# A gated Mamba block with a ternary feed-forward layer: the mean and variance of nine row tiles computed by ScalarE's accumulator in place of VectorE's batch-norm instructions

## What is computed

```python
def _layernorm(x, eps=1e-05):
    m = jnp.mean(x, axis=-1, keepdims=True); v = jnp.var(x, axis=-1, keepdims=True)
    return (x - m) / jnp.sqrt(v + eps)
# selective scan on ctx (4 x 512 x 256), gated by z = layernorm(x):
#   u = silu(causal_conv(ctx @ in_proj)), dt = softplus(...), B, C = rows of x_proj(u)
#   state = state * exp(dt * A) + (dt * u) * B ;  y = sum_n state_n * C_n  (16 states n, 512 channels)
x = x + tanh(g_xattn) * (y + D * u) * silu(z)
# ternary feed-forward layer, F = 2048: bitlinear(v, w) = quant8(rmsnorm(v)) @ ternary(w).T
h = silu(bitlinear(layernorm(x), w_gate)) * bitlinear(layernorm(x), w_up)
x = x + tanh(g_ffn) * bitlinear(h, w_down)
```

## Time and profile before

| what | us |
|---|---|
| three executions | 660.37, 652.05, 660.92 (median 660.37) |
| the profiled execution, whole time | 652.9 |
| its span, first to last instruction | 651.0 |
| what lies around the span | 1.9 |
| mean granted TensorE clock in it | 0.942 of full speed |

### The profile page before, as it was taken

How to read it: one execution, slowest core, us unless ns; L and a number is a source line. 1 busy time by engine, 2 the same in 40 slices (tenths; PEclk the granted TensorE clock), 3 DMA queues, 4 the chain that set the end, 5 groups by cost and what they waited for, 6 DMA issues and landing times. The chain is left out here.

```text
span 651.0 us, 9055 instructions
## 1 busy us (share of the span) xinstructions
PE 508.2 (78%) x2966; PEld 344.2 (53%) x2966; DVE 573.6 (88%) x796; ACT 501.3 (77%) x711; POOL 511.1 (79%) x281
## 2 busy tenths in 40 slices
PE   6998576876757577878778778787678777889996
PEld 2443264765645455656556556565456555654552
DVE  1879999999989999998989999999999999985642
ACT  3989699796977696969586868696878787766874
POOL 1534999999989999999999899999899989821000
PEclk9999777869788999899978998999998999999999
DMA  9993910711830101027301010183010010000000
GB/s 300 397 411 83 384 34 32 259 49 55 327 104 1 48 2 34 32 80 310 97 12 55 12 35 21 53 332 128 5 39 27 33 33 18 2 33 1 16 34 33
DMA packets 29985, 64.47 MB, mean 99 GB/s; under 512 B 3681, under 2 KB 11873, under 8 KB 26866
## 3 DMA queue, kind: packets, MB, share of 16 engines
q1 hardware_dynamic: 29938, 63.89, 27.4%
HBM read 55.75 MB, written 8.13 MB: 98 GB/s over the span
## 5 line engine op out<-in xcount | busy, mean ns | idle before, releaser
L669 POOL TENSOR_TENSOR area_s<-area_s,b_bc 128x1024 f32<-128x1024 f32 x128 | 300.7, 2363 | 21.6 <-DVE u_all L1159 16.9
L423 PE MATMUL pY<-ident,area_s 128*128 128x128 f32 x640 | 107.5, 296 | 81.2 <-DVE area_s L1167 79.9
L423 PEld LDWEIGHTS pY<-ident,area_s 128*128 128x128 f32 x640 | 76.5, 149 | 110.9 <-DVE area_s L1167 76.3
L878 ACT ACTIVATE pA<-dt_all,a_neg 128x512 f32<-128x512 f32 x160 | 107.8, 682 | 23.4 <-DVE area_s L1159 14.5
L463 PE MATMUL pG<-wq_gu,area_f 128*128 128x512 fp8e4 x448 | 112.6, 392 | 7.7 <-ACT area_f L844 5.6
L1159 DVE TENSOR_TENSOR_SCAN area_s<-pA,area_s 128x512 f32<-128x512 f32 x96 | 114.3, 1204 | 3.8 <-ACT pA L878 3.7
L1167 DVE TENSOR_TENSOR area_s<-area_s,pC 128x512 f32<-128x512 f32 x144 | 95.3, 664 | 9.8 <-issue 6.4
L661 POOL TENSOR_TENSOR u_all<-u_all 128x1024 f32<-128x1024 f32 x44 | 103.9, 2361 | 0.0
L417 PE MATMUL pC<-ident,xdT 128*128 128x128 f32 x576 | 94.5, 293 | 1.4 <-DVE xdT L1035 1.3
L417 PEld LDWEIGHTS pC<-ident,xdT 128*128 128x128 f32 x576 | 74.7, 150 | 6.1 <-DVE area_s L1167 3.4
L463 PEld LDWEIGHTS pG<-wq_gu,area_f 128*128 128x128 bf16 x448 | 43.5, 101 | 54.4 <-ACT area_f L844 7.6
(11 more groups left out here) (156 smaller groups left out, 960.0 us busy)
## 6 DMA issues: line engine op xcount, KB each, us to landing
b_bc<-bc_rows SPq DMA_DIRECT2D x16, 1024.0 KB, 7.5
area_s<-x SPq DMA_DIRECT2D x32, 256.0 KB, 3.0
u_all<-bc_rows SPq DMA_DIRECT2D x14, 512.0 KB, 5.9
b_bc<-w_gate SPq DMA_DIRECT2D x1, 4096.0 KB, 14.5
dt_all<-x SPq DMA_DIRECT2D x1, 4096.0 KB, 24.8
area_f<-w_up SPq DMA_DIRECT2D x1, 4096.0 KB, 34.2
area_f<-w_down SPq DMA_DIRECT2D x1, 4096.0 KB, 15.1
out<-area_f SPq DMA_DIRECT2D x16, 256.0 KB, 2.1
```

The lines of the kernel that those rows point to most:

```text
L423: mm = pe.matmul(pY[:, k * P:(k + 1) * P], src[:, k * P:(k + 1) * P], ident[:, :], is_transpose=True, start=(first and k == 0), stop=(last ...
L669: gp.tensor_tensor(db[c % NDB], du[s % 2].rearrange("p (a l) -> p a l", a=1).to_broadcast([P, CH, L]), b_bc[:, CH * c:CH * c + CH, :], ALU ...
L878: act.activation(exp_bank(s, n), dt_all[:, s, :], ACT.Exp, scale=a_neg[:, s % NT, n:n + 1]).then_inc(S["s_exp"], 1)
```

## The change

For nine tiles (t = 1, 2, 3, 5, 6, 7, 9, 10, 11) the statistics move from DVE to ACT. Tiles 0, 4, 8 and 12 to 15 keep `stats` on DVE (`own_stats`). For the nine:

- `x_sum(t)`, new: an ACT Copy over the 128 x 512 tile whose accumulator gives the sum. It stands at n = 3 of the step before the tile's own, and at n = 6 where t1 is a multiple of 4.
- `centre(t)` takes the sum as its bias and writes 512 times (mean - x). It moves from n = 10 to n = 8 (behind the two copies of hqT there), and stays at n = 10 where t1 is a multiple of 4.
- `x_deviation(t)`, new: an ACT Square over xn with accumulator, and a Copy of the 128 x 1 result with scale and offset into VE. It stands at n = 9, or at n = 10 right behind `centre`. The factor 512 cancels, since the root is of the scaled variance.
- `x_rstd(t)` on POOL moves behind `dt_u(s + 1)`, or behind `times_b(s + 1, 0)` where t1 is a multiple of 4, and waits for the new semaphore f_ve.
- The elementwise outputs of `x_sum` and `x_deviation` go to `nobody`, which is the space of w_xp_sb, used last in the first part of the kernel.

```diff
+def own_stats(t):
+    return t % NT == 0 or t >= UNITS - NT
+BN_AT = [sum(own_stats(i) for i in range(t)) for t in range(UNITS + 1)]
...
             def x_rstd(t):
-                gp.wait_ge(S["f_bn"], 3 * t + 3)
+                gp.wait_ge(S["f_ve"], t + 1)
...
-                if t1 % NT and (t1 + 1) % NT:
-                    x_rstd(t1 + 1)
                 times_c(s, 1)
-                if t1 % NT == 0:
-                    x_rstd(t1 + 1)
                 times_b(s, NDB + 3)
                 if s + 1 < UNITS:
                     dt_u(s + 1)
+                if t1 % NT and (t1 + 1) % NT:
+                    x_rstd(t1 + 1)
+                if s + 1 < UNITS:
                     times_b(s + 1, 0)
+                if t1 % NT == 0:
+                    x_rstd(t1 + 1)
...
+                    act.wait_ge(S["f_sum"], t - BN_AT[t] + 1)
+                    act.activation(out, tile_x1(t), ACT.Identity, scale=-float(D), bias=col(XSUM)).then_inc(S["f_xn"], 1)
+            def x_sum(t):
+                act.wait_ge(S["s_x1"], (t // NT) * NT + NT)
+                act.wait_ge(S["f_xn"], t)
+                past(act, S["f_dev"], t - BN_AT[t])
+                act.activation(nobody, tile_x1(t), ACT.Copy, accum_out=col(XSUM)).then_inc(S["f_sum"], 1)
+            def x_deviation(t):
+                act.wait_ge(S["f_xn"], t + 1)
+                act.wait_ge(S["f_sum"], t - BN_AT[t] + 1)
+                act.activation(nobody, xn.rearrange("p (a c) -> p a c", a=NT), ACT.Square, accum_out=col(DEV)).then_inc(S["f_dev"], 1)
+                act.wait_ge(S["f_dev"], t - BN_AT[t] + 1)
+                act.wait_ge(S["f_rr"], t)
+                act.activation(col(VE), col(DEV), ACT.Copy, scale=(1.0 + RMS_EPS) / D, bias=RMS_EPS * LN_EPS * D * D).then_inc(S["f_ve"], 1)
...
-                    if n == 10 and (t1 + 1) % NT:
+                    if n == (3 if t1 % NT else 6) and (t1 + 1) % NT:
+                        x_sum(t1 + 1)
+                    if n == (8 if t1 % NT else 10) and (t1 + 1) % NT:
                         centre(t1 + 1)
+                    if n == (9 if t1 % NT else 10) and (t1 + 1) % NT:
+                        x_deviation(t1 + 1)
...
-                    if n == (4 if t1 % NT else 8) and (t1 + 1) % NT:
-                        stats(t1 + 1)
```

More of the change, by code:

```diff
@@ L60 @@
 C_STEP = {2: 3, 3: 4, 6: 7, 7: 11, 10: 12, 11: 13, 14: 15, 15: 16}
-VE, RR, M2, REC1, XS, SS, RH, M3, REC2, FAC, MH = range(11)
+def own_stats(t):
+    return t % NT == 0 or t >= UNITS - NT
+BN_AT = [sum(own_stats(i) for i in range(t)) for t in range(UNITS + 1)]
+VE, RR, M2, REC1, XS, SS, RH, M3, REC2, FAC, MH, XSUM, DEV = range(13)
 CS, EC, OSC = (14, 15), (16, 17), (18, 19)
@@ L72 @@
     s_exp s_dbu s_scan s_mul s_pmul s_pytr s_cb s_ytr s_du s_skip s_skd s_sz s_szp s_szT s_y s_x1
-    f_bn f_rr f_xn f_xs f_e f_xm f_xqp f_xqT f_gate f_silu f_up f_h f_sq f_mh f_rh f_hs f_hm
+    f_bn f_sum f_dev f_ve f_rr f_xn f_xs f_e f_xm f_xqp f_xqT f_gate f_silu f_up f_h f_sq f_mh f_rh f_hs f_hm
     f_hqp f_hqT f_dn f_o""".split()
@@ L168, in build @@
         rows = [zt[:, :], szT[:, :], zn[:, :], zt[:, :]]
+        nobody = w_xp_sb[:, :, :]
         z_buf = [zn, zt]
@@ L829, in centre @@
             def centre(t):
-                act.wait_ge(S["f_bn"], 3 * t + 2)
                 past(act, S["f_xqp"], t)
-                act.activation(xn.rearrange("p (a c) -> p a c", a=NT), tile_x1(t), ACT.Identity, scale=-1.0, bias=mv[:, 0:1]).then_inc(S["f_xn"], 1)
+                out = xn.rearrange("p (a c) -> p a c", a=NT)
+                if own_stats(t):
+                    act.wait_ge(S["f_bn"], 2 * BN_AT[t] + 2)
+                    act.activation(out, tile_x1(t), ACT.Identity, scale=-1.0, bias=mv[:, 0:1]).then_inc(S["f_xn"], 1)
+                else:
+                    act.wait_ge(S["f_sum"], t - BN_AT[t] + 1)
[12 more added lines that the diff above has]
+                act.activation(col(VE), col(DEV), ACT.Copy, scale=(1.0 + RMS_EPS) / D, bias=RMS_EPS * LN_EPS * D * D).then_inc(S["f_ve"], 1)
             def scale_x(t):
@@ L1095, in stats @@
                 dve.wait_ge(S["s_x1"], (t // NT) * NT + NT)
+                i = 2 * BN_AT[t]
                 dve.bn_stats(st6, tile_x1(t)).then_inc(S["f_bn"], 1)
-                dve.wait_ge(S["f_bn"], 3 * t + 1)
+                dve.wait_ge(S["f_bn"], i + 1)
                 past(dve, S["f_xn"], t)
                 dve.bn_aggr(mv, st6).then_inc(S["f_bn"], 1)
-                dve.wait_ge(S["f_bn"], 3 * t + 2)
+                dve.wait_ge(S["f_bn"], i + 2)
                 past(dve, S["f_rr"], t)
-                dve.tensor_scalar(col(VE), mv[:, 1:2], 1.0 + RMS_EPS, RMS_EPS * LN_EPS, ALU.mult, ALU.add).then_inc(S["f_bn"], 1)
+                dve.tensor_scalar(col(VE), mv[:, 1:2], 1.0 + RMS_EPS, RMS_EPS * LN_EPS, ALU.mult, ALU.add).then_inc(S["f_ve"], 1)
             def x_scales(t):
```

## The result

| | before | after |
|---|---|---|
| median of 20 executions each, us | 653.09 | 658.74 |
| lowest to highest | 650.98 to 660.92 | 654.43 to 661.86 |
| profiled execution, its span | 652.9, 651.0 | 657.33, 655.5 |
| mean granted TensorE clock in it | 0.942 | 0.940 |

The changed kernel takes 1.0062 times the time of the one before, 95% interval 1.0038 to 1.0087: slower by a little more than half a per cent, and within 2%. Between the two profiled executions the difference is 4.4 us, where the sum of the prediction gave 3.4. The predicted time was 663.8 us, 5.1 above the measured median, inside the range of 648 to 671.

A forecast was written before the change was run, and what follows sets the result against it. DVE and ACT were taken to hand each step to each other, ACT's packed row leaving it no slack; per-step net delays summed to 3.4 us, which added to the 660.37 median gave 663.8 us, range 648 to 671.

The forecast's parts named there:

- Rival 1: Whole kernel: DVE's 9.2 us gain comes through, time 651.2 us, or 643.7 on the profiled execution's level; chance 0.18.
- Rival 2: ACT's packed row: all added work exposed, DVE waiting at scans of states 11 and 12; 16.8 us, 677.2; chance 0.10.
- Rival 4: On ACT: Copy or Square needs another table, two loads per `x_deviation`, 23.0 us in all, time 683.4; chance 0.02.
- How the sum stands to the runs: Whole kernel: 3.4 us added to the profiled 652.9 gives 656.3, and to the three-run median 660.37 gives 663.8.
- The two prices: On ACT, per moved tile: `x_sum` costs 0.83 us and `x_deviation` 1.04 us.
- The sum of steps: Steps 4 to 6, 8 to 10, 12 to 14: net delays of state 14's exponential, together 3.4 us.
- DVE's part: ACT's wait for a scan, taken back by DVE's earlier scan: 0.25 us in step 9, 0.60 in step 14.
- the slack of 0.65: Steps 10, 13, less markedly 6: ACT's wait for PE, 1.22 us against step 5's 0.57, hides a late Silu.
- `x_deviation` is not hidden: Step 8: forecast had it hidden by ACT's 1.86 us wait for PE, 1.29 more than step 5; net +0.55.
- the slack of 0.34: Step 12: ACT's wait for PE, 0.91 against 0.57 us, was subtracted from the added work; net +0.96.
- Rival 3: PE idles longer and its clock falls in all nine steps, 5.9 us on top of 3.4, time 669.7; chance 0.10.

## Why the prediction was right, and where not

**The direction and its cause: right.** Nine times 1.02 us off the busiest engine did not make the kernel faster, because ACT's packed row up to the table load sets the step, and `x_deviation` stands in it. Rival 1 would have shown steps 5, 9 and 14 about 1 us shorter; step 5 is 0.14 shorter, 9 is 1.15 and 14 0.12 longer. Rival 2's sign does appear (in step 6 of the changed kernel with repeats DVE waits 0.67 us for an exponential at 267.88, in front of the scan of state 11), but the scans of states 12 and 13 don't wait, and that of state 14 waits for the row behind the table load as before, so its price of 16.8 us does not come. Rival 4's extra table loads are not there: the groups of after have 16 and 13 loads by the two lines of the block's loop, like before. The scan of state 14 in step 5 started at 23.50 (forecast about 23.6), ACT's wait of 1.00 us is gone, and POOL meets VE ready at `x_rstd` of all nine tiles. On the page DVE is 6.7 us less busy and ACT 11.4 more, where I had forecast 9 and 17. By durations the forecast holds: the three groups of `stats` fell from 10.9, 2.9 and 2.5 to 4.8, 1.3 and 1.1 us, 9.1 together, and the new rows of ACT above add up to 16.5. Both page totals moved by less, as they would if the overlap of two instructions is counted once.

**The predicted time: the step that failed is "How the sum stands to the runs".** The sum belonged to the profiled execution, 652.9 + 3.4 = 656.3, and there 657.33 was measured. I carried it to the median of three, 660.37, because two of three lay near 660.7. Twenty executions put the median at 653.09, and three of the twenty are above 659; the changed kernel's are at 658.74. Forecast against the final median of before, 663.8 is 1.6% slower, where 0.62% [0.38, 0.87] was measured. The base was 660.37 - 653.09 = 7.3 us too high and the change by medians 5.65 - 3.4 = 2.2 too small; that the two partly cancel, and the time is off by 5.1 only, is luck. Which terms of the change were too small, the table of steps below says.

**The two prices: too high.** `x_deviation` is 0.86 us instead of 1.04. `x_sum` is 613 ns and its accumulator read overlaps the next instruction; in step 5 the three start at 222.13, 222.66 and 222.75, so it costs 0.62 instead of 0.83, below the lower bound of 0.67 that I had taken from a quarter of the square. The read that I had put at 0.22 costs 0.09 from start to start where the next instruction does not need its result, as behind `x_sum`; behind the square, where the column waits for it, it is 235.43 - 235.19 = 0.24.

**The sum of steps: near, by errors that cancel.** The terms of the prediction and the same step at the raised clock (changed less before, both with PE's repeats; the mean clocks of each pair differ by 0.02 at most):

| step | forecast | measured | what failed |
|---|---|---|---|
| 5 | +0.04 | -0.11 | price |
| 9 | +0.79 | +0.48 | price, and DVE's part 0.1 larger, by the overlap |
| 6, 10, 13 | +0.14 each | +0.48, +0.48, +0.51 | the slack of 0.65 is none |
| 14 | +0.44 | +0.11 | price, DVE's part |
| 4 | +0.21 | +0.98, table load +0.12 | little at the table load; the rest is where the low clock falls |
| 8 | +0.55 | +0.85 | `x_deviation` is not hidden |
| 12 | +0.96 | +0.81 | price, and the slack of 0.34 |

These make 0.04 + 0.79 + 0.42 + 0.44 + 0.21 + 0.55 + 0.96 = 3.4 against 4.6, of which 0.86 is step 4's time behind the table load; without it the change itself makes 3.7. In steps 6, 10, 13 and 8 the failed reading is the same: waits of ACT for PE in the earlier trace rows (0.42 and 0.80, 1.06 and 0.80) were taken as room for later ACT work. In the profile they belong to the low clock of those steps; at full clock they are one wait of 0.57 that moves with the table load. In before's step 8 the table load stands at 334.47 - 315.9 = 18.6 us, as at the raised clock, and the step is 36.33 instead of 34.28: what the lower clock adds lies behind it. In the changed kernel's step 8, at a clock of 0.82, it lies in part ahead: PE waits 3.47 us instead of 2.85 for the copies of hqT, its transposes then run at a clock of 0.50, and the table load stands at 20.72 instead of 19.40 with the repeats.

**Rival 3, the clock: not the cause of the loss, but the noise in it.** The mean clock of after is 0.940 against 0.942 in the two profiled executions. The loss stays at 4 to 6 us with and without PE's repeats, and in steps 6, 9 and 10, at a clock of 1.00 on both sides, it is 0.48 us each. What goes with the clock is that steps 4, 8 and 12 take lengths 1.5 to 2.0 us apart in kernels whose program there is the same. How much of the loss between the medians without repeats is of this kind, no run separates.

Step 14 keeps 0.70 of DVE's 1.02 us on its path where step 6 keeps 0.37, because ACT's wait for the scan there is 0.61 in the one and 0.26 in the other. What stays open is why these waits differ. Steps 7 and 11 took 0.3 to 0.4 us more in one or the other of the kernels with repeats, with a clock of 0.97, and are not explained by the change.

## What to carry to other kernels

Work taken from the busiest engine pays only where that engine sets the end of a wait; follow the one row that everything after it moves with (here ACT's table load), and price the addition by the starts in that row. A wait is slack only if its releaser doesn't itself wait for the engine that waits: see what PE's product had been waiting for before you spend ACT's wait for it. And before two profiles are compared step by step, compare the granted clock of each step, and take the base of a forecast from the execution that the durations come from.

## What the hardware did that I had not expected

In this kernel a wait of the matmul engine cost more than its own length. Repeating PE's own transposes in front of its waits (2.85 us in step 8), more work by every count (PE's matmuls go from 2966 to 3098), made the kernel before 0.85% faster [0.5%, 1.2%], and its 8 executions lie within 2.6 us instead of ten. And the accumulator of `x_sum` on ACT costs little: the instruction with it takes 613 ns and the read 186, but the next instruction starts 0.09 us behind the read's start.
